# Cross-attention and FFN block, projection stage: features of x loaded by tokens, the layer norm's scale put behind the query products, values stored in rows of 2 KB

## The reference

```
xn = layernorm(x)                                   # over the 512 features, no gain, no bias
q = xn @ Wq.T + bq;  k = ctx @ Wk.T + bk;  v = ctx @ Wv.T + bv
s = q k^T / sqrt(32);  s = where(mask == 0, -1e9, s) + bias
x = x + softmax(s) v @ Wo.T + bo
x = x + ffn(layernorm(x))     # router of 256, top 8, plus gelu(z @ W1.T) @ W2.T, hidden width 2048
```

## Time and profile before

| | us |
|---|---|
| median of 3 runs | 1788.86 (1784.54 to 1789.95) |
| the profiled execution: its time | 1783.78 |
| its span, first to last instruction | 1782.0 |
| TensorE busy in the span | 1765.0 (99%) |
| VectorE, ScalarE, GpSimd busy | 1225.4, 906.1, 967.7 |
| granted TensorE clock, mean | 0.999 of full |

### The profile page before, as it was taken

How to read it: one execution, slowest core, us unless ns; L and a number is a source line. 1 busy time by engine, 2 the same in 40 slices (tenths; PEclk the granted TensorE clock), 3 DMA queues, 4 the chain that set the end, 5 groups by cost and what they waited for, 6 DMA issues and landing times.

```text
span 1782.0 us, 34024 instructions
## 1 busy us (share of the span) xinstructions
PE 1765.0 (99%) x11952; PEld 1366.3 (77%) x11952; DVE 1225.4 (69%) x2779; ACT 906.1 (51%) x2030; POOL 967.7 (54%) x466
## 2 busy tenths in 40 slices
PE   9999999999999999999999999999999999999999
PEld 7888886555555555555788888888888888888888
DVE  7565557999999999999757555555654556645553
ACT  4322226999999999999434232322423124232231
POOL 1423247999999999998546243233332333423331
PEclk9999999999999999999999999999999999999999
DMA  9997999536345436330578785865948659477584
GB/s 333 318 325 269 315 315 360 174 119 220 114 137 196 141 97 237 96 131 19 192 240 298 236 272 157 308 201 183 324 128 307 205 183 325 150 265 243 161 281 144
DMA packets 221479, 388.52 MB, mean 218 GB/s; under 512 B 15488, under 2 KB 71424, under 8 KB 220800
## 3 DMA queue, kind: packets, MB, share of 16 engines
q1 hardware_dynamic: 217760, 373.23, 62.6%
q0 software_dynamic: 3264, 12.58, 1.9%
q10 hardware_dynamic: 288, 0.52, 0.1%
HBM read 310.78 MB, written 75.50 MB: 217 GB/s over the span
## 4 chain that ended last, share of the span: by engine, by line
PE 50%; DVE 1%; issue 0%; POOL 0%; ACT 0%; DVEq 0%; ACTq 0%
PE banks L2026 20%; PE banks L2000 18%; PE banks L1899 7%; PE banks L1938 5%; PE banks L1893 1%; DVE k_x L1454 0%; DVE h_q L1615 0%; DVE k_x L1625 0%; DVE n_stats L1461 0%; DVE n_zo L1447 0%; DVE k_az L1477 0%; POOL n_rstd L1361 0%; DVE n_g_l L1447 0%; DVE n_u L1583 0%; DVE n_sel L1593 0%
## 5 line engine op out<-in xcount | busy, mean ns | idle before, releaser
L2000 PEld LDWEIGHTS banks<-n_zo,n_w 128*128 128x128 f32 x2688 | 500.4, 189 | 64.8 <-DVE h_bias L1738 2.2
L2000 PE MATMUL banks<-n_zo,n_w 128*128 128x256 f32 x2688 | 533.5, 282 | 2.4 <-DVE h_bias L1738 2.0
L1383 POOL TENSOR_TENSOR n_g_l<-h_pos,n_g_h 128x512 fp32r<-128x512 f32 x128 | 196.4, 1534 | 558.5 <-DVE n_g_h L1632 558.5
L2026 PE MATMUL banks<-n_w,n_g_h 128*128 128x512 f32 x1024 | 383.7, 394 | 0.0
L1100 ACT ACTIVATE l_tiles<-l_tiles,l_small 128x512 f32<-128x512 f32 x376 | 267.2, 715 | 0.1
L1034 DVE CUSTOM_DVE_ANT_0 l_tiles<-banks,l_tiles 128x512 f32<-128x512 f32 x353 | 224.8, 687 | 25.7 <-PE banks L936 24.6
L947 PEld LDWEIGHTS banks<-ident,l_tiles 128*128 128x128 f32 x1524 | 163.3, 141 | 90.1 <-issue 70.5
L947 PE MATMUL banks<-ident,l_tiles 128*128 128x128 f32 x1524 | 207.4, 279 | 1.0 <-ACT a_pT L1078 0.9
L2026 PE MATMUL banks<-n_w,n_g_l 128*128 128x512 f32 x512 | 202.0, 394 | 0.0
L2026 PEld LDWEIGHTS banks<-n_w,n_g_h 128*128 128x128 f32 x1024 | 193.3, 189 | 8.1
L1041 DVE COPY a_pT<-banks 128x512 f32<-128x512 f32 x256 | 164.4, 683 | 5.0 <-PE banks L947 3.1
(11 more groups left out here) (255 smaller groups left out, 3476.5 us busy)
## 6 DMA issues: line engine op xcount, KB each, us to landing
n_w<-wf_d SPq DMA_DIRECT2D x448, 256.0 KB, 3.6
n_w<-w_d SPq DMA_DIRECT2D x112, 512.0 KB, 4.5
a_pos<-pos_d SPq DMA_DIRECT2D x16, 1024.0 KB, 5.6
l_bias<-in_bias POOLq DMA_DIRECT2D x9, 1024.0 KB, 8.2
l_tiles<-in_x SPq DMA_DIRECT2D x8, 1024.0 KB, 10.3
l_bias<-in_mask SPq DMA_DIRECT2D x8, 1024.0 KB, 13.1
k_d<-l_tiles SPq DMA_DIRECT2D x8, 1024.0 KB, 11.6
pos_d<-l_bias SPq DMA_DIRECT2D x8, 1024.0 KB, 10.8
```

The lines of the kernel that those rows point to most:

```text
L1383: pool.tensor_tensor(out=g_l[:, j % NG, :], in0=g_f[:, j % NG, :], in1=g_h[:, j % NG, :].bitcast(F32), op=ALU.subtract).then_inc(g_low, 1)
L2000: last = pe.matmul(bank, w1[:, q % NR, m, k * P:(k + 1) * P], zo[:, j, MOVING[i], k, :], start=s == 0 and i in (P1, P6, P5), stop=s == NPP ...
L2026: last = pe.matmul(ps_y[:, t, :], (g_h, g_l)[i][:, j % NG, t * P:(t + 1) * P], w2[:, j % NG, k, :], start=f == 0 and m == 0, stop=f == NF ...
```

## The change

The transposes are gone. x is given a second time, features by tokens (`xT`), and loaded into the tile that held `xn`; its high part comes from there on ScalarE (`turned_high`, ahead of the key evictions from batch 1 on), its low part on VectorE. The mean is taken out of Wq once: VectorE sums the four chunks of Wq, TensorE sums over partitions with a product of ones in fp32 (`weight_means`, after V1 of batch 0), VectorE subtracts the mean before Wq is split. 1/deviation is spread over the partitions as the mask factor was, but as a high and a low part, so there are three row products per batch instead of one, with three sets of four diagonal instructions. ScalarE copies the row (`keep_row`), and each query chunk is now finished by two VectorE instructions instead of one: times the row of 1/deviation (`scale_queries`, which frees the bank), then plus bias, times mask factor (`mask_queries`). In batch 0 all four of the first kind come before the four of the second. Values go out in one transfer of 2 KB rows, and `attend` reads them with rows of 512 bytes out of these.

```diff
+            def load_xT(b):
+                sp.dma_start(xT_raw[:, :, :], tokens(xT[b])).then_inc(xT_in, 16)
...
                     load_c(b + 1)
-                    sp.wait_ge(xn_done, NT * (b + 1))
+                    sp.wait_ge(stats_done, NT * (b + 1))
                     load_x(b + 1)
                 sp.wait_ge(k_done, NC * (b + 1))
                 store_qk(b, k_s, k_d, k_out)
+                if more:
+                    sp.wait_ge(xT_low, NC * (b + 1))
+                    load_xT(b + 1)
...
-                for c in range(NC):
-                    sp.dma_start(tokens(v_d[B * c + b]), v_s[:, :, c * P:(c + 1) * P]).then_inc(v_out, 16)
+                sp.dma_start(tokens(v_d[b]), v_s[:, :, :]).then_inc(v_out, 16)
                 if more:
-                    sp.wait_ge(bank_free, NPB + NVQ * (b + 1))
+                    sp.wait_ge(q_done, NC * (b + 1))
                     store_qk(b, q_s, q_d, q_out)
...
             load_weight(1)
+            sp.wait_ge(piece_low, 2 * NC)
+            load_xT(0)
             sp.wait_ge(w_low, NC)
...
             def first_mask_tile():
...
-                pool.wait_ge(xn_done, NT * B)
+                pool.wait_ge(stats_done, NT * B)
...
+            def diagonal(v):
+                for t in range(NT):
+                    dve.tensor_scalar(fac_diag[:, t, :], ident[:, :], v[:, t:t + 1], None, ALU.mult) \
+                        .then_inc(diag_done, 1)
+            def add_weights():
...
+                dve.tensor_tensor(out=w_sums, in0=raw[:, 0:2, :], in1=raw[:, 2:4, :], op=ALU.add).then_inc(w_mean, 1)
...
+                dve.tensor_tensor(out=w_sum, in0=w_sums[:, 0, :], in1=w_sums[:, 1, :], op=ALU.add).then_inc(w_mean, 1)
+            def centre_weights():
...
+                for c in range(NC):
+                    dve.scalar_tensor_tensor(out=raw[:, c, :], in0=ps_t[:, 2, :], scalar=-1.0 / D, in1=raw[:, c, :],
+                                             op0=ALU.mult, op1=ALU.add).then_inc(w_mean, 1)
+                dve.tensor_scalar(bq_c[:, :], bq_c[:, :], QSCALE, None, ALU.mult).then_inc(w_mean, 1)
+            def scale_queries(b, c):
...
+                dve.tensor_tensor(out=q_s[:, c, :], in0=ps_j[:, n % NPB, :], in1=fac_row[:, :], op=ALU.mult) \
+                    .then_inc(bank_free, 1)
+            def mask_queries(b, c):
...
+                dve.scalar_tensor_tensor(out=q_s[:, c, :], in0=q_s[:, c, :], scalar=bq_c[:, c:c + 1],
+                                         in1=fac_copy.bitcast(F32),
+                                         op0=ALU.add, op1=ALU.mult).then_inc(q_done, 1)
...
                 dve.wait_ge(rstd_done, b + 1)
-                for t in range(NT):
-                    dve.tensor_scalar(xn[:, t, :], x_raw[:, t, :], mv[:, t, 0:1], rstd[:, t:t + 1],
-                                      ALU.subtract, ALU.mult).then_inc(xn_done, 1)
+                dve.tensor_copy(r_h.bitcast(F32R), rstd[:, :]).then_inc(fac_done, 1)
+                dve.wait_ge(fac_done, NFAC * b + R_HIGH)
+                dve.tensor_tensor(out=r_l, in0=rstd[:, :], in1=r_h, op=ALU.subtract).then_inc(fac_done, 1)
+                diagonal(r_h)
                 if b == 0:
                     weight_low(0)
+                    add_weights()
...
+                dve.wait_ge(fac_turned, NFAC * b + R_HIGH)
+                diagonal(r_l)
+                if b == 0:
+                    centre_weights()
                     weight_low(1)
-                    values(b, 1, 2)
+                    values(b, 1, NT)
...
+            def turned_high(b):
+                need(act, projected, NPJ * b)
+                act.wait_ge(xT_in, 16 * (b + 1))
+                for c in range(NC):
+                    act.activation(xT_h[:, c, :], xT_raw[:, c, :], ACT.Copy).then_inc(xT_high, 1)
+            def keep_row(b):
+                act.wait_ge(fac_turned, NFAC * b + R_LOW)
+                act.activation(fac_row[:, :], ps_t[:, 1, :], ACT.Copy, scale=QSCALE).then_inc(fac_row_done, 1)
...
                 if b == 0:
                     weight_high(0)
+                else:
+                    turned_high(b)
                 act.wait_ge(k_out, 16 * (b + 1))
...
+            def row_product(b, part):
+                pe.wait_ge(diag_done, NT * (NFAC * b + part) + 1)
...
+                pe.matmul(ps_t[:, 0 if part == FAC else 1, :], ones_r[:, :],
+                          fac_diag[:, :, :].rearrange("p t n -> p (t n)"),
+                          start=part != R_LOW, stop=part != R_HIGH).then_inc(fac_turned, 1)
+            def weight_means():
+                pe.wait_ge(w_mean, SUMMED)
+                pe.matmul(ps_t[:, 2, :], ones[:, :], w_sum, start=True, stop=True).then_inc(w_mean, 1)
...
-                    for t in range(NT):
-                        last = pe.transpose(ps_t[:, c, t * P:(t + 1) * P], xn[:, t, c * P:(c + 1) * P],
-                                            ident[:, :])
-                    last.then_inc(x_turned, 1)
+                if b > 0:
+                    row_product(b, R_HIGH)
                 for t in range(NT):
...
+                    if b == 0 and t in (0, 2):
+                        row_product(b, R_LOW if t else R_HIGH)
+                    if b == 0 and t == 1:
+                        weight_means()
+                    if b > 0 and t == 0:
+                        row_product(b, R_LOW)
                 if b > 0:
-                    factors(b)
+                    row_product(b, FAC)
...
-                    if b == 0 and c == 1:
-                        factors(b)
+                    if b == 0 and c == NC - 1:
+                        row_product(b, FAC)
...
             def load_v(g, j):
-                sp.dma_start(v[:, j, :, :], tokens(v_d[NG * g + j])).then_inc(v_in[j], 16)
+                c, b = divmod(NG * g + j, B)
+                sp.dma_start(v[:, j, :, :], tokens(v_d[b])[:, :, c * P:(c + 1) * P]).then_inc(v_in[j], 16)
```

More of the change, by code:

```diff
@@ L63, in build @@
             late = Late(nc, early, banks)
-            project(nc, ident, ones, neg_half, x, ctxT, mask, WqT, bq, WkT, bk, WvT, bv, W1T,
+            project(nc, ident, ones, neg_half, x, xT, ctxT, mask, WqT, bq, WkT, bk, WvT, bv, W1T,
                     q_d, k_d, v_d, pos_d, wf_d, bias, WoT, wo_d, ahead, late)
@@ L157, in walk_rounds, with project @@
         step(rounds, j, False)
-def project(nc, ident, ones, neg_half, x, ctxT, mask, WqT, bq, WkT, bk, WvT, bv, W1T,
+def project(nc, ident, ones, neg_half, x, xT, ctxT, mask, WqT, bq, WkT, bk, WvT, bv, W1T,
             q_d, k_d, v_d, pos_d, wf_d, bias, WoT, wo_d, ahead, late):
@@ L172, in project @@
         wf_h, wf_l = sb("wf_h", [P, 2, 2, D], F32R), sb("wf_l", [P, 2, 2, D], F32R)
-        x_raw, xn, k_s = late.tiles
+        x_raw, xT_raw, k_s = late.tiles
         c_raw, m_raw, pos = late.bias
@@ L198, in project @@
         mv = late.small[:, NT * 6:NT * 8].rearrange("p (t n) -> p t n", t=NT)
+        r_h, r_l = late.small[:, 0:NT], late.small[:, NT:2 * NT]
+        fac_copy = fac_diag[:, :, :].rearrange("p t n -> p (t n)")
+        w_sums, w_sum = q_s[:, 0:2, :], q_s[:, 2, :]
         var_e = sb("var_e", [P, NT])
@@ L532, in body @@
                 dve.tensor_scalar(q_fac[:, :], pos_min[:, :], 0.0, None, ALU.is_equal).then_inc(fac_done, 1)
[L533 to L537 removed]
+                dve.wait_ge(fac_done, NFAC * b + FAC)
+                dve.wait_ge(fac_turned, NFAC * b + R_LOW)
+                diagonal(q_fac)
+                if b > 0:
+                    values(b, 0, NT)
                 if more:
                     context_low(b + 1)
[L540 removed]
+                dve.wait_ge(fac_row_done, 2 * b + R_ROW)
+                if b == 0:
+                    for c in range(NC):
+                        scale_queries(b, c)
                 for c in range(NC):
[L543 to L549 removed]
+                    if b > 0:
+                        scale_queries(b, c)
+                    mask_queries(b, c)
                     if not more and c % 2 == 0:
@@ L565, in weight_high @@
                 for c in range(NC):
+                    if k == 1:
+                        act.wait_ge(w_mean, MEANS + c + 1)
                     act.activation(w_h[n][:, c, :], raw[:, c, :], ACT.Copy).then_inc(w_high, 1)
+            def turned_high(b):
+                need(act, projected, NPJ * b)
+                act.wait_ge(xT_in, 16 * (b + 1))
+                for c in range(NC):
+                    act.activation(xT_h[:, c, :], xT_raw[:, c, :], ACT.Copy).then_inc(xT_high, 1)
+            def keep_row(b):
+                act.wait_ge(fac_turned, NFAC * b + R_LOW)
+                act.activation(fac_row[:, :], ps_t[:, 1, :], ACT.Copy, scale=QSCALE).then_inc(fac_row_done, 1)
             def context_high(b):
@@ L580, in body @@
                         .then_inc(k_done, 1)
-                for c in range(NC):
-                    act.wait_ge(x_turned, NC * b + c + 1)
-                    act.activation(xT_h[:, c, :], ps_t[:, c, :], ACT.Copy).then_inc(xT_high, 1)
```

(4 more changed lines are left out.)

99 lines of the change are left out of this document (49 added, 50 removed).

## The result

The changed kernel takes 1793.5 us (median of 19 runs, 1790.25 to 1795.78). Beside it the kernel before took 1788.86 (19 runs, 1784.52 to 1792.83). The medians are 4.6 us apart (1.0026). The comparison's own ratio, which is not that of the medians, is 1.0034, with a 95% interval of 1.0025 to 1.0042. So the change makes the kernel slower, by an amount at the edge of the 5.4 us that the prediction took as the least to be told from no change. The forecast was 1793.2. The profiled execution took 1790.85, which is 7.0 more than the profiled one of before.

A forecast was written before the change was run, and what follows sets the result against it. TensorE, 99% busy, was taken as the bound. Start +5.6, clock +1.7, batches 2 to 6 -6.7, batch 7 +3.2 and attention's first tiles +0.5 gave +4.3 on 1788.86, so 1793.2 us, range 1784 to 1800.

The forecast's parts named there:

- A middle batch: Batches 2 to 6: transposes go, two row products come, TensorE does not wait; 1.35 us less each, -6.7 in all.
- Rival D: Each batch's row product waits for its diagonal, so the saved 1.35 us are lost; +11, 1800 us, chance 0.04.
- Batch 0: Later Wo copy, GpSimd's low part and the mask addend delay the query steps; batch 1 starts at 43.45, loss 2.15 us.
- Batch 1: TensorE waits 4.8 us (3 to 7) before the first value product, for key evictions behind ScalarE's W1 parts and copies.
- My bound from the transfers: Batch 1: an extra megabyte in a full queue lands W1 2.7 us later, alone making the first value product 3.7 late.
- The clock behind that wait: TensorE at half clock after batch 1's wait, the lower level of 1.2 GHz; +1.7 us, between 0 and 3.5.
- Batch 7: VectorE's mask steps with two SBUF inputs wait for GpSimd's mask tiles; stage's end +3.2 us, bounds -1 to +5.
- Rival B: Only batch 7 is free: its mask steps don't clash with GpSimd, +0.7 there; total +1.8, 1790.7 us, chance 0.23.
- Attention's first tiles: Start of attention: first value tiles arrive behind a longer transfer queue, 0 to 3 x 2.4 us later; taken as +0.5.
- The median: Whole kernel: the earlier median, 5.1 us above its profiled run, taken as base; 1788.86 + 4.3 = 1793.2 us.
- A (the gain comes through): ScalarE's queue has cover at batch 1, so only batch 0's +1.0 stays; -7.8, 1781 us, chance 0.1.
- C (the transfer queue decides): From batch 5 on, with attention's tiles in the queue, the context lands too late; +10, 1799 us, chance 0.13.

The follow-up runs named there:

- e1: Changed kernel with ScalarE's four W1 high parts of batch 0 made behind batch 1's key evictions; 1791.89 us, ratio 1.0026 to the kernel before.
- e7: Changed kernel with xT loaded in batch 0 only, later batches using the same tile again; 1792.42 us, ratio 1.0030 to the kernel before.
- a0: Changed kernel run again without any edit, beside e10; 1794.52 us (5 runs), ratio 1.0046 to the kernel before.
- e3: Changed kernel plus 12 matmuls with unused result at the end of the projections; 1790.92 us, ratio 1.0022 to the kernel before.
- e9: Kernel before plus 12 matmuls with unused result at the end of its projections; 1787.39 us, ratio 1.0003 to the kernel before.
- e10: As e1, with SyncE issuing batch 2's context and x loads at the end of batch 0; 1786.62 us, ratio 1.0001 to the kernel before.
- e11: e10 plus 10 matmuls with unused result at the end of the projections; 1783.15 us, ratio 0.9984 to the kernel before.
- e6: Changed kernel with ScalarE's four high copies of x behind the key evictions in every batch; 1815.5 us, ratio 1.0167 to the kernel before.

## Why the prediction was right, by its steps

- **A middle batch: right.** 33.38 us against 33.32 worked out, in all five, with no wait of TensorE. Rival D is out. The DMA share was 0.91, not 0.94, and VectorE's busy time 24.8, not about 23, since mask steps beside GpSimd's low parts take up to 1.77 instead of 0.75; the slack bore it.
- **Batch 0: right, step by step.** GpSimd's low part of Wo ended at 36.07, forecast 35.8; the mask addend, held by it from 33.08 on, at 37.15, forecast 37.0; the keys of batch 1 started at 43.54, forecast 43.45. That the last agrees within 0.1 us is luck, as other traces of the same batch 0 have it from 42.8 to 45.2.
- **Batch 1: right in size (5.00, forecast 4.8), half right in its reason.** ScalarE's order was as told: the W1 parts and the copies ahead of the evictions, and e1 removed the gap. What started the chain was not `root(1)` alone: it ended at 52.03, and the sums waited 1.03 more for W1, so that the eviction came 0.5 later than I had it. My bound from the transfers, W1 not ahead of 50.5, had a wrong reason and was 2.5 short. e7 shows that a megabyte less ahead of it changes nothing there; the rows show W1 issued 5.4 later, behind the stores of the addend and of Wo in SyncE's queue. I had costed the addend's clash for VectorE and not for the queue behind it.
- **The clock behind that wait: right in this trace.** 1.6, forecast 1.7 from the earlier trace rows. In a0 the windows of the same place give 2.9, and in e1, behind a gap of 3.94, 3.0; so a price from one pair of windows was at the low end. The trace agrees with the Trainium skill, TensorE: Matmul & The Clock Gate, What's actually happening, that an idle TensorE falls to the lower of its two clocks.
- **Batch 7: right.** +3.2 forecast, +3.0 measured from its first key product to VectorE's last step. The mask step behind Q1 took 3.18. The first mask tile held the split for 4.57, and TensorE waited 1.5 us in all for the two diagonals behind it; the query products started 0.8 later than before, counted from the batch's start (275.31 - 250.73 against 273.07 - 249.30), where I had 0.5. Rival B rested on mask steps that don't clash; they do. The trace agrees with the lock between GpSimd and two SBUF inputs that the page SBUF — State Buffer of the Trainium skill names (SBUF: two separate sides).
- **Attention's first tiles: the mis-sized term.** I took +0.5 for value tiles behind a longer queue. The start of attention cost +2.0, and not through transfers. VectorE now ends 1.6 us after TensorE's last transposes of the stage (291.94 against 288.90 + 1.47), where before it ended half a microsecond before them (287.51 against 288.03); the stages' gap grew from 1.55 to 3.84, and behind it the clock halved. The lower clock is nearly all of the +2.0: from attention's first product to the first one with the values it is 10.67 us instead of 8.86, and 8.87 in e3 with the gap filled. I had the rule and the price from batch 1 and did not ask it of the next gap. That is most of what lies between the sum, +4.3, and the profiled +7.0.
- **The median.** 1788.86 + 4.3 came out at 1793.2 against 1793.5 because the runs of before lie in two groups and their median was in the upper one, 5.1 above the profiled execution, while the changed kernel has one group. In the later comparison with the changed kernel the difference was 6.9 (1794.52 against 1787.65), as in the profile. So the forecast was nearer than its sum deserved. That before's upper group lost clock is on record, run by run; that it lost it at attention's start fits e9's narrow spread but is not shown.
- **Rivals.** A (the gain comes through) needed cover at batch 1 that wasn't there. With two queues reordered, e10 is level with the kernel before and e11, with unused products added, some 3 to 4.5 us below it; A had priced 7.8 below. C (the transfer queue decides) is refuted by e7.

## What to carry to other kernels

When an engine is given new work ahead of a step that frees a buffer, follow every in-order queue that hangs on it, the one that issues transfers too: here moving ScalarE's work alone only moved the wait into SyncE's order, and both had to be reordered to get the 6 us back. Ask of each new gap on TensorE what the clock behind it costs, and of each end of a stage which engine arrives last. Here the step that was moved from a PSUM input onto two SBUF inputs came to wait for GpSimd, where the old one had not been seen to.

## What the runs showed of the hardware

- Idle times of 3.8 to 5.0 us on TensorE each left windows at a granted clock of 0.50 to 0.69, the lower level being 1.2 GHz; so did one of 2.73 (e6: 0.55 and 0.60). Unused products in the gap kept it at 1.00, and at a gap of 1.55 the profiled run stayed at 1.00. The same kernel lost 1.6 us by the windows in one trace and 2.9 in another.
- VectorE instructions were held while a GpSimd instruction ran: a conversion of four elements per partition took 4.57 (0.17 alone) and ended with it; the mask addend took 4.07 (1.21 alone) and a mask step of two SBUF inputs 3.18 (0.75 alone), and ended 1.08 and 0.55 behind it. Beside GpSimd's four low parts of W1 in a row, a mask step took 0.92 to 1.77, and the four low parts 6.50 together in batch 6 (5.59 in batch 6 of the kernel before).
- Values in rows of 512 bytes or of 2 KB: no difference (1.0002, 0.9993 to 1.0010).
